# Row sums and the FFN LayerNorm statistics of a four-stage transformer block, computed on GpSimd instead of VectorE

## Time and profile before

| | |
|---|---|
| median of 3 runs | 191.12 us (190.76 to 191.35) |
| profiled execution, whole | 190.59 us |
| its span (first to last instruction) | 188.4 us |
| PE busy | 177.7 us, 94% |
| DVE busy | 149.4 us, 79% |
| ACT busy | 111.2 us, 59% |
| POOL busy | 48.6 us, 26% |
| granted TensorE clock | 1.00 throughout |

### The profile page before, as it was taken

How to read it: one execution, slowest core, us unless ns; L and a number is a source line. 1 busy time by engine, 2 the same in 40 slices (tenths; PEclk the granted TensorE clock), 3 DMA queues, 4 the chain that set the end, 5 groups by cost and what they waited for, 6 DMA issues and landing times.

```text
span 188.4 us, 3886 instructions
## 1 busy us (share of the span) xinstructions
PE 177.7 (94%) x1270; PEld 157.6 (84%) x1270; DVE 149.4 (79%) x472; ACT 111.2 (59%) x257; POOL 48.6 (26%) x65
## 2 busy tenths in 40 slices
...
DMA packets 9825, 5.96 MB, mean 32 GB/s; under 512 B 447, under 2 KB 9422, under 8 KB 9806
## 3 DMA queue, kind: packets, MB, share of 16 engines
...
q10 hardware_dynamic: 720, 0.47, 1.0%
...
## 4 chain that ended last, share of the span: by engine, by line
PE 74%; DVE 14%; issue 4%; ACT 3%; DMA 2%; POOL 1%; DVEq 0%; ACTq 0%; POOLq 0%
PE bank_o L1117 15%; PE bank_m L1047 12%; PE bank_p L1105 7%; PE bank_s L907 6%; PE bank_s L909 5%; PE bank_s L908 5%; PE bank_h L907 3%; PE bank_h L909 3%; PE bank_h L908 3%; PE bank_m L942 3%; PE bank_h L978 2%; DVE rsin L384 2%; DVE xn L699 2%; DMA id_sb<-in_ident 2%; DVE stat L677 1%
## 5 line engine op out<-in xcount | busy, mean ns | idle before, releaser
L1117 PE MATMUL bank_o<-vone,pt 128*128 128x128 f32 x272 | 35.9, 274 | 0.0
L1117 PEld LDWEIGHTS bank_o<-vone,pt 128*128 128x128 f32 x272 | 34.3, 191 | 0.9
L1047 PE MATMUL bank_m<-wd,hid 128*128 128x128 f32 x256 | 32.2, 276 | 0.6 <-DVE y L769 0.4
L1047 PEld LDWEIGHTS bank_m<-wd,hid 128*128 128x128 f32 x256 | 30.9, 192 | 2.0 <-DVE y L769 0.8
L473 POOL TENSOR_SCALAR veps<-mom 128x4 f32<-128x4 f32 (+2 forms) x19 | 7.1, 371 | 96.3 <-DVE mom L681 96.0
L611 ACT ACTIVATE relu<-bank_h 128x512 f32<-128x512 f32 (+1 forms) x40 | 20.0, 511 | 11.0 <-PE bank_h L909 9.5
L666 ACT COPY pt<-bank_p 128x512 f32<-128x512 f32 (+3 forms) x31 | 16.1, 531 | 13.1 <-PE bank_p L1105 12.9
L789 DVE SCALAR_TENSOR_TENSOR spiked<-y,spiked 128x512 bf16<-128x512 f32 (+1 forms) x36 | 22.1, 613 | 0.6
L907 PE MATMUL bank_s<-kh,qh 128*128 128x512 f32 (+3 forms) x43 | 17.7, 412 | 0.9 <-ACT vone L646 0.4
L677 DVE BATCH_NORM_STATS2 stat<-xs 128x6 f32<-128x128 f32 x64 | 14.2, 281 | 3.5 <-DMA xs<-in_x 3.4
L657 ACT ACTIVATE kphi<-kphi,negm 128x1024 f32<-128x1024 f32 (+4 forms) x12 | 11.3, 938 | 7.0 <-DVE negm L866 7.0
...
## 6 DMA issues: line engine op xcount, KB each, us to landing
...
hid<-in_w_qkv ACTq DMA_DIRECT2D x1, 192.0 KB, 4.1
```

The source lines that it names most:

```text
L1047: last = nc.tensor.matmul(MB[:, C * t:C * t + C], hid[:, j % 2, m, P * t:P * t + P], wd[:, m, :], start=(m == 0), stop=(m == M - 1))
L1117: last = nc.tensor.matmul(O[:, C * (i % TG):C * (i % TG) + C], pt[:, n % 3, P * b:P * b + P], v[:, k, :], start=(k == 0), stop=(k == i))
```

## The change

Two computations leave VectorE for GpSimd, and the four instruction tables (PE, ACT, DVE, POOL) are written out anew.

First, `row_sum-i` (16 steps): DVE's `tensor_reduce` and `reciprocal` become a GpSimd `tensor_tensor` add (row tiles 9 to 15) and a `pow` with exponent -1. Second, for norms 1 and 3 (11 jobs), DVE does `bn_stats` alone; GpSimd merges the even and odd halves that `bn_stats` leaves, `var = (M2_even + M2_odd)/128 + (mean_even - mean_odd)^2 / 4`, in six small instructions, and then the `pow` as before. The mean is not needed there. Norms 0 and 2 stay as they were.

```diff
@@ GpSimd, step rstd
-                    pool.wait_ge(mom_ready[n], g + 1)
-                    nc.gpsimd.tensor_scalar_add(veps[:, n, ts], mom[:, n, ts, 1], EPS_LN).then_inc(veps_ready[n], 1)
+                    if n % 2:
+                        pool.wait_ge(bn_done[n], g + 1)
+                        near, apart = mom[:, n, ts, 0], mom[:, n, ts, 1]
+                        nc.gpsimd.tensor_tensor(apart, stat[:, n, ts, 1], stat[:, n, ts, 4],
+                                                ALU.subtract).then_inc(apart_ready[n], 1)
+                        nc.gpsimd.tensor_tensor(near, stat[:, n, ts, 2], stat[:, n, ts, 5],
+                                                ALU.add).then_inc(near_ready[n], 1)
+                        pool.wait_ge(apart_ready[n], 3 * g + 1)
+                        nc.gpsimd.tensor_tensor(apart, apart, apart, ALU.mult).then_inc(apart_ready[n], 1)
+                        pool.wait_ge(near_ready[n], 2 * g + 1)
+                        nc.gpsimd.tensor_scalar(near, near, 1.0 / C, EPS_LN, ALU.mult, ALU.add).then_inc(near_ready[n], 1)
+                        pool.wait_ge(apart_ready[n], 3 * g + 2)
+                        nc.gpsimd.tensor_scalar(apart, apart, 0.25, None, ALU.mult).then_inc(apart_ready[n], 1)
+                        pool.wait_ge(apart_ready[n], 3 * g + 3)
+                        pool.wait_ge(near_ready[n], 2 * g + 2)
+                        nc.gpsimd.tensor_tensor(veps[:, n, ts], apart, near, ALU.add).then_inc(veps_ready[n], 1)
+                    else:
+                        pool.wait_ge(mom_ready[n], g + 1)
+                        nc.gpsimd.tensor_scalar_add(veps[:, n, ts], mom[:, n, ts, 1], EPS_LN).then_inc(veps_ready[n], 1)
@@ GpSimd, new step
+                elif step[0] == "row_sum":
+                    i = step[1]
+                    np_ = len(exp_pieces(i))
+                    pool.wait_ge(e_ready, piece_no[i, np_ - 1] + 1)
+                    total = psums[:, i, 0:1]
+                    if np_ > 1:
+                        total = psum_all[:, i:i + 1]
+                        nc.gpsimd.tensor_tensor(total, psums[:, i, 0:1], psums[:, i, 1:2], ALU.add).then_inc(ps_ready, 1)
+                        pool.wait_ge(ps_ready, sum(len(exp_pieces(k)) > 1 for k in range(i + 1)))
+                    pool.wait_ge(consts, 1)
+                    nc.gpsimd.tensor_tensor(rsum[:, i:i + 1], total, mone[:, 0:1], ALU.pow).then_inc(rs_ready, 1)
@@ VectorE, step stats
                     last.then_inc(bn_done[n], 1)
+                    if n % 2:
+                        continue
                     dve.wait_ge(bn_done[n], g + 1)
...
@@ VectorE, step row_sum
-                        nc.vector.tensor_reduce(total, psums[:, i, 0:np_], AX_X, ALU.add).then_inc(ps_ready, 1)
...
-                    nc.vector.reciprocal(rsum[:, i:i + 1], total).then_inc(rs_ready, 1)
@@ PLAN, a piece of the table of POOL
-centre ids rstd-0-0 rstd-0-1 w_lo-0 rstd-0-2 bias-0 rstd-0-3 rstd-1-0 bias-1 sq-0-0 bias-2 sq-1-0 vnext_zero rstd-1-1
+vnext_zero rstd-0-0 centre rstd-0-1 w_lo-0 rstd-0-2 rstd-0-3 ids bias-0 rstd-1-0 sq-0-1 bias-1 bias-2 rstd-1-1
...
```

More of the change, by code:

```diff
@@ L120 @@
     "pe": """
[L121 to L134, removed]
-pv-13-0 pv-13-1 f1-7-3 pt-13-3 s-15-0 pv-13-2 pv-13-3 pt-14-0 s-15-1 pt-14-1 pt-14-2 turn-3-3 s-15-2 pv-14-0 f1-8-0
```

108 lines of the change are left out of this document (58 added, 50 removed).

## The result

The changed kernel takes 188.53 us (median of 4 runs, 188.38 to 188.88) against 191.23 us before (4 runs, 190.76 to 191.35): ratio 0.9863, 95% interval 0.9839 to 0.9887. The forecast was 190.2 with a range from 188.9: the sign was right, the gain is 2.7 us where 0.9 was forecast, and the time lies 0.4 us under the range. The profiled executions stand at 190.59 (span 188.4) and 188.38 (span 186.6), so they differ by 2.2 us only: that of before lay 0.64 us under its median, that of after 0.15 under.

A forecast was written before the change was run, and what follows sets the result against it. PE bounds 88 to 180 us, a DVE and ACT chain 55 to 88. The terms +0.5 - 0.55 - 0.85 + 0 = -0.9 us took the profiled 190.59 to 189.7; plus 0.53, forecast 190.2 us, range 188.9 to 192.0.

The forecast's parts named there:

- A: First FFN, 32 to 48 us: longer GpSimd chains delay lo-1-3, which PE needs; +0.5 us, range 0 to +1.8.
- B: First rotary, 55 to 65 us: rsin product no longer beside a GpSimd square; -0.55 us, bounds -0.85 and +0.3.
- C: Second rotary and first row tiles, 65 to 88 us: matmuls fill PE's wait; -0.85 us, range -1.5 to +0.3.
- D: The rest, from o-5 to xf-10; forecast 0 from 88 us on, range -0.3 to +0.7.
- the last line of the sum: Whole kernel: profiled 190.59 us becomes 189.7; adding the median's 0.53 us above the profile gives 190.2 us.
- The +0.3 for `sq-3-3`: First rotary: this square, put on ACT between two copies, delays cos-0 by 0.3 us.
- From 88 us on: 0: Behind 88 us PE's work covers row sums, queues and the longer last chain; 0, range -0.3 to +0.7 us.
- PE as the bound: Rival: PE has 92 us without a gap, so no change, 191.1 us; chance 0.25.
- GpSimd as the bound in the first FFN: Rival: chain instructions cost 0.47 us each, PE stands 1.8 us at f1-3-0; slower, 192.2 us; chance 0.14.
- The small GpSimd instructions: Rival: between 32 and 88 us 30 new ones hold up DVE, adding 2.3 us; slower, 192.5 us; chance 0.06.
- More comes: Rival: PE's 3.65 us open in 55 to 88 us closes except 1.0 and 0.5; 188.9 us; chance 0.10.

The follow-up runs named there:

- fill: Kernel before with f2-4 and the scores of row tile 2 ahead of the second Q, K transposes on PE; 191.33 us beside 191.35.
- bias_later: Kernel before with GpSimd's ids and bias-0 moved behind rstd-0-3; 191.37 us, ratio 0.9990.
- square_off: Kernel before with the square sq-4-0 moved from GpSimd to ScalarE, right behind relu-4-0; 190.42 us beside 191.35.
- order_placed: New order with the old arithmetic, with spike-0-3 behind heads-3, spike-4-0 behind o-1 and row_sum-15 ahead of stats-3-4; 189.92 us.
- rows_placed: Changed kernel with row sums back on VectorE, spike-4-0 behind o-1 and row_sum-15 ahead of stats-3-4; 188.81 us.
- stats_back: Changed kernel with only bn_aggr of norms 1 and 3 back on VectorE and the short chain on GpSimd; 189.38 us.
- five: Changed kernel with five GpSimd instructions in place of six in each merged group; 188.65 us.
- second_merged: Changed kernel with the first FFN's LayerNorm statistics merged on VectorE again (bn_aggr), the second's left on GpSimd; 189.06 us.
- chain_longer: Changed kernel with nine more small GpSimd instructions in each of the first FFN's five statistics chains; median 194.33 us, 193.16 in the traced run.
- first_merged: Changed kernel with the second FFN's LayerNorm statistics merged on VectorE again (bn_aggr), the first's left on GpSimd; 189.15 us.
- moves_alone: Old instruction tables with the new arithmetic, row sums and merging on GpSimd; 192.55 us, ratio 1.0073.

## Why the prediction was wrong, step by step

By the table the gain splits as follows, where "usual before" takes the start column of `fill`, `bias_later` and `square_off` (24.26 on average) and the rest of before:

| | forecast | measured | of it order | merging | row sums |
|---|---|---|---|---|---|
| start | not in the sum | -0.97 | -0.86 | -0.11 | 0 |
| A | +0.5 | -0.29 | -0.08 | -0.21 | 0 |
| B | -0.55 | -0.92 | -0.74 | -0.17 | -0.01 |
| C | -0.85 | -0.71 | -0.65 | -0.03 | -0.03 |
| D | 0 | +0.08 | +0.92 | -0.61 | -0.23 |
| sum | -0.9 | -2.8 | -1.4 | -1.1 | -0.3 |

(order: `order_placed` less usual before; merging: `rows_placed` less `order_placed`; row sums: after less `rows_placed`. The -0.11 at the start is no effect of the merging: nothing of it runs there, and traces of the new order differ by so much.) The medians give the same sums: some 191.35 to 189.92, 188.81 and 188.53. Three limits go with the table. The gains of the two moves overlap, so their shares hang on which goes first: from `order_placed` over `stats_back` (189.38) the row sums give 0.5 and the merging 0.85, 1.4 together as before. The order's entries in A and B are good in their sum only, since the cut between them shifts. And `o-5` stands 1.00 to 1.32 us behind the end of `pv-5` on PE, as the kernel goes, so C and D are good to some 0.3 us: from the end of `pv-5` to that of `pv-15` PE takes 81.58 us before, 82.33 in `order_placed`, 82.04 in `rows_placed` and 81.64 after.

- **The first failed step is the last line of the sum**, "the median was 0.53 us above it". The prediction carried the distance between profile and median over to the changed kernel as if it were noise. It was the hold-up of `xn` by `bias-0`, which the new order takes away (`bias-0` at 14.59, and `norm-0-3` behind a later step on DVE). It is a third of the gain. With it the forecast would have been 189.25 (191.12 - 0.97 - 0.9); the 0.7 us that then remain are mainly term A.
- **Term A failed in sign.** The chain was rightly seen and its price rightly bounded (1.43 us for the first, near the 1.4 of the lower end, and 2.57 for the last). The queue ended a little sooner than reckoned: `lo-1-3` was over at 45.77 us and not at 46.3, 1.3 us before `f1-3-0`. So nothing of the +0.5 came, and `five`, with one instruction less in each chain, gains nothing either, while DVE's relief in A, which the prediction left out, is worth 0.2 there and 0.2 in B (`second_merged`). `chain_longer` shows that the rival's danger was real, only farther off. (The prediction counts one group of `bn_aggr` that leaves DVE between 55 and 88 us; the trace of before has two, at 57.20 and 87.53.)
- **Term B was right in kind**: `rsin` 2.06 to 1.22 us, and `square_off` gives 0.93 by itself. The +0.3 for `sq-3-3` did not appear, and 0.2 of merging came on top.
- **Term C was near in size and wrong in reason.** Filling the wait brings nothing (`fill`). 0.3 of it comes with the square off POOL (31.63 to 31.34 in `square_off`); what in the new order brings the other 0.4 was not isolated.
- **"From 88 us on: 0" was right as a sum and wrong as an argument.** Under the old order it holds: with the moves alone D is 87.23, as before. The new order has D at 88.12 without the moves, so there DVE does count, and merging and row sums give back 0.84. "PE busy 92.0 of 92.0 us" could not show this: in `first_merged` too PE shows as busy for 77.90 of the 78 us from 100 us on, and yet it lost the 0.26 us at 139.62 above.
- **The rivals.** PE as the bound and GpSimd as the bound in the first FFN did not come; the latter came true in part under the old order (`moves_alone`, A +1.6, of which 0.6 at POOL's `xl`). The small GpSimd instructions held up nothing: they are the ones that wait. The `pow` at 59.58 took 2.08 us beside two DVE products that took 1.23 and 1.22, their usual time. "More comes" was the nearest with 188.9, but by luck: it let PE's open time between 55 and 88 us shrink from 3.65 to 1.5 us, and 2.3 us of it are left, while 1.3 of the 2.8 us of gain lie ahead of that stretch, in the start and A.

The rule of the Trainium skill, page "SBUF — State Buffer", section "Who interferes with whom", was weighed for the rotary's product and for the new small instructions, and not for the other long ones. That section also says that a VectorE instruction with at most one SBUF input stays out of the contention unless it runs in a mode that takes both ports, that `tensor_scalar` can enter such a mode, and that whichever issues first blocks the other wholly. For GpSimd's instructions of 512 columns the places looked at here agree: `xn` and `spiked<-y` (`tensor_scalar`, one input in SBUF; no run shows their mode) and the squares, comparisons and products (two inputs in SBUF) last until `bias`, `xl` or the square is over, while `xs<-bank_s,xs`, with one of its two inputs in PSUM, took its usual 0.69 us at 36.19 with `bias` running until 37.33.

None of the runs beats the changed kernel; `five` and `rows_placed` are within 0.3 us of it.
